# Start addresses 32 bytes further on: experts' tokens, context and the first half's query weights in SBUF

## The reference

```
x = x + latent_attention(context, layernorm(x))      # 8 heads of 128; keys and values from context and latents together
x = x + ffn(layernorm(x))                            # 256 -> 1024 -> 256, gelu, and a small term made of 16 of the tokens
x = x + cross_attention(layernorm(x), context)       # one head of 256
x = x + experts(layernorm(x))                        # 8 experts, each 256 -> 256 gate and up, silu(gate) * up, 256 -> 256 down
```

## Time and profile before

| | us |
|---|---|
| median of three executions | 1987.82 |
| lowest and highest | 1985.39, 1988.81 |
| the profiled execution: its own time | 1991.09 |
| the profiled execution: its span, first to last instruction | 1989.3 |

### The profile page before, as it was taken

The page is one execution under the profiler, slowest core; times in us unless marked ns, Lnnn a source line. Parts: engine busy times, 40 slices in busy tenths (PEclk is TensorE's granted clock), DMA queues, the critical chain, the costliest instruction groups (busy, mean ns, idle before and its releaser), DMA issues.

```text
span 1989.3 us, 41475 instructions
## 1 busy us (share of the span) xinstructions
PE 1927.2 (97%) x14078; PEld 1803.2 (91%) x14078; DVE 1367.9 (69%) x3408; ACT 1115.5 (56%) x2334; POOL 407.1 (20%) x650
## 2 busy tenths in 40 slices
PE   7999999999999999999987899999999999999998
PEld 6788888888888888888886899999999999999998
DVE  7877776776777776776746566766666666766665
ACT  5655565555655565555655655554555555544553
POOL 2222222222222222222213511111111101111100
PEclk9999999999999999999999999999999999999999
DMA  4000000000000000000012200000000000000000
GB/s 162 12 22 21 11 11 21 21 21 5 16 21 21 11 11 21 21 21 6 10 34 89 67 15 15 12 17 17 11 16 16 17 12 17 12 17 12 17 7 12
DMA packets 47211, 44.51 MB, mean 22 GB/s; under 512 B 6848, under 2 KB 45376, under 8 KB 47168
## 3 DMA queue, kind: packets, MB, share of 16 engines
q1 hardware_dynamic: 47168, 43.96, 6.9%
HBM read 34.77 MB, written 8.39 MB: 22 GB/s over the span
## 4 chain that ended last, share of the span: by engine, by line
PE 83%; DVE 7%; ACT 5%; issue 3%; POOL 1%; SPq 1%; DMA 0%; DVEq 0%; ACTq 0%; POOLq 0%
PE ring L618 9%; PE ring L620 9%; PE ring L619 9%; PE ring L1820 7%; PE ring L1818 7%; PE ring L1819 7%; PE ring L671 4%; PE sim L1818 3%; PE sim L1819 3%; PE sim L1820 3%; PE sim L618 3%; PE sim L620 2%; PE sim L619 2%; PE ps_x L1818 2%; PE ps_x L1820 2%
## 5 line engine op out<-in xcount | busy, mean ns | idle before, releaser
L411 ACT ACTIVATE a_pr<-sim,a_nmax 128x512 f32<-128x512 f32 x256 | 174.5, 689 | 208.4 <-DVE a_nmax L537 208.3
L1818 PE MATMUL ring<-b_xch,b_weh 128*128 128x256 f32 x1024 | 289.5, 283 | 1.7 <-DVE b_act_e L1464 1.7
L1819 PE MATMUL ring<-b_xcl,b_weh 128*128 128x256 f32 x1024 | 285.7, 279 | 0.0
L1820 PE MATMUL ring<-b_xch,b_wel 128*128 128x256 f32 x1024 | 285.6, 279 | 0.0
L326 POOL TENSOR_SCALAR a_pr<-a_pr,a_rinv 128x512 f32<-128x512 f32 x256 | 183.1, 729 | 498.3 <-DVE a_rinv L547 495.4
L1818 PEld LDWEIGHTS ring<-b_xch,b_weh 128*128 128x128 f32 x1024 | 192.3, 188 | 1.9 <-DVE b_act_e L1464 1.9
L1819 PEld LDWEIGHTS ring<-b_xcl,b_weh 128*128 128x128 f32 x1024 | 193.0, 188 | 0.0
L1820 PEld LDWEIGHTS ring<-b_xch,b_wel 128*128 128x128 f32 x1024 | 192.1, 188 | 0.0
L1464 DVE TENSOR_TENSOR b_act_e<-b_act_e,ring 128x512 f32<-128x512 f32 x128 | 87.9, 687 | 116.7 <-PE ring L1820 102.4
L528 DVE TENSOR_TENSOR a_ptl<-ring,a_pth 128x512 fp32r<-128x512 f32 x256 | 163.9, 682 | 3.1 <-ACT a_pth L401 2.0
L515 DVE SCALAR_TENSOR_TENSOR a_ktl<-ring,a_bkv_s,a_kth 128x512 fp32r<-128x512 f32 x128 | 95.3, 744 | 102.1 <-ACT a_kth L391 102.1
(11 more groups left out here) (378 smaller groups left out, 6246.0 us busy)
## 6 DMA issues: line engine op xcount, KB each, us to landing
a_c_in<-in_ctx_in SPq DMA_DIRECT2D x16, 256.0 KB, 2.6
a_x_in<-in_x SPq DMA_DIRECT2D x16, 256.0 KB, 2.9
a_x_res<-in_x SPq DMA_DIRECT2D x16, 256.0 KB, 2.6
x_between<-a_x_out SPq DMA_DIRECT2D x16, 256.0 KB, 2.2
b_x_s<-x_between SPq DMA_DIRECT2D x16, 256.0 KB, 2.6
b_up<-b_ev SPq DMA_DIRECT2D x256, 1.0 KB
out_x<-b_acc SPq DMA_DIRECT2D x16, 256.0 KB, 2.2
b_ct_raw<-in_ctxT SPq DMA_DIRECT2D x15, 256.0 KB, 2.6
```

The costliest lines, as they stand in the source:

```text
L411: nc.scalar.activation(pr[:, h % 2, t, :], sim[t][:], ACT.Exp, bias=nmax[:, h % 2, t:t + 1], accum_out=rsum[:, h % 2, t:t + 1]).then_inc(e ...
L1818: nc.tensor.matmul(out, lh, rh, start=(n == 0), stop=False)
L1819: nc.tensor.matmul(out, lh, rl, start=False, stop=False)
L1820: last = nc.tensor.matmul(out, ll, rh, start=False, stop=(n == len(parts) - 1 and not more))
```

## The change

`put` takes fractions of `odd`, and six tiles are put at half a step, that is 32 bytes behind a multiple of 128. Instructions, waits and their order are the same.

```
         if odd is not None:
-            self.top = (self.top - 64 * odd + 127) // 128 * 128 + 64 * odd
+            behind = int(64 * odd)
+            self.top = (self.top - behind + 127) // 128 * 128 + behind
...
-    (raw_q, wql), wqh = of["w_queries"].put("a_wql", ..., odd=1), of["w_queries"].put("a_wqh", ..., odd=1)
+    (raw_q, wql), wqh = of["w_queries"].put("a_wql", ..., odd=0.5), of["w_queries"].put("a_wqh", ..., odd=0.5)
...
-    cth, (wq_raw, ctl) = put("w_queries", "cth", ..., odd=0), put("w_queries", "ctl", ..., odd=0)
+    cth, (wq_raw, ctl) = put("w_queries", "cth", ..., odd=0.5), put("w_queries", "ctl", ..., odd=0.5)
...
-    xch, xcl = (put("values0", n, [P, DC, S], F32R, odd=0) for n in ("xch", "xcl"))
+    xch, xcl = (put("values0", n, [P, DC, S], F32R, odd=0.5) for n in ("xch", "xcl"))
```

More of the change, by code:

```diff
@@ L179, in latent_attention @@
         "a_wvl", [P, DC, INNER], F32R, raw=True, odd=0)
-    (raw_q, wql), wqh = of["w_queries"].put("a_wql", [P, DC, INNER], F32R, raw=True, odd=1), of["w_queries"].put(
-        "a_wqh", [P, DC, INNER], F32R, odd=1)
+    (raw_q, wql), wqh = of["w_queries"].put("a_wql", [P, DC, INNER], F32R, raw=True, odd=0.5), of["w_queries"].put(
+        "a_wqh", [P, DC, INNER], F32R, odd=0.5)
     (raw_k, wkl), wkh = of["w_keys"].put("a_wkl", [P, DC, INNER], F32R, raw=True, odd=1), of["w_keys"].put(
@@ L821, in ffn_attention_experts @@
         "w_queries", "wvl", [P, DC, D], F32R, raw=True, odd=1)
-    cth, (wq_raw, ctl) = put("w_queries", "cth", [P, DC, S], F32R, odd=0), put(
-        "w_queries", "ctl", [P, DC, S], F32R, raw=True, odd=0)
+    cth, (wq_raw, ctl) = put("w_queries", "cth", [P, DC, S], F32R, odd=0.5), put(
+        "w_queries", "ctl", [P, DC, S], F32R, raw=True, odd=0.5)
     once = {"K": (wk_raw, mh, ml), "Q": (wq_raw, cth, ctl), "V": (wv_raw, wvh, wvl)}
```

## The result

The changed kernel takes 1999.72 us (median of 5 runs, 1997.68 to 2003.08); the kernel before took 1987.82 beside it (5 runs, 1985.39 to 1989.78). The ratio is 1.0063, with a 95% interval of 1.0047 to 1.008: about 12 us slower, where 12 us faster had been forecast. The profiled span is 1997.9 us, against 1989.3.

What follows compares the result with a forecast made beforehand. PE's matmuls were taken as the bound: their number times the step from start to start. Terms of 10.6 + 1.7 + 1.2 + 0.3 = 13.8 us, 12 kept, gave 1979.1, or 1975.8 at the median; forecast 1976, range 1958 to 2000.

Steps and rivals of the forecast that it cites:

- slower, the phase is lost the other way: Rival for the moved products: with 32 bytes between the streams the fast phase no longer exists; middle 2000 us, chance 0.26.
- two prices, 1994 and 2012: The slower rival's times: fast strings fall to 118 ns (5.8 us), or the third, slower speed becomes the rule (24 us).
- step 1: Gate and up, tokens from 0 to 32: 2304 slow matmuls go from 117.9 to 113.3 ns, saving 10.6 us.
- step 2: First half's query weights, from 64 to 32: half of 768 matmuls are slow and become fast, saving 1.7 us.
- step 3: Context, from 0 to 32: score matmuls save 1.2 us, values at most 0.3 us.
- step 4: Neighbouring tiles that move along, such as b_act_e: DVE's product takes 687 ns and has idle time; counted as nothing.
- not the residue alone: Claim on what sets the speed: strings with the same residues modulo 128 run at 117.9 and 113.3 ns.
- The warning at the end: Matmuls of unmoved tiles (down, w1, attention's outputs) should keep their steps; if not, the sum by tiles is wrong.
- The rule weighed there: PE has two independent read ports, moving operand and weights, so the start address within 128 bytes should change nothing: 0.

Runs made afterwards that it cites:

- m1: Separate kernel without the computation: strings of equal 256-column products for every pair of starts, moving and stationary, in 32-byte steps modulo 256; steps 113.3 to 120.0 ns.
- t1: Kernel before with only the tokens b_xch and b_xcl moved to 32 bytes behind a multiple of 128; 1996.29 us, ratio 1.004.
- t3: Kernel before with only the first half's query weights a_wql and a_wqh moved to 32; 1992.45 us, ratio 1.0018.
- t8: Kernel before with the context b_cth, b_ctl at 160 modulo 256, and b_v_b, b_rt, b_wr moved with it; 1988.58 us, ratio 0.9991.
- m3: Separate kernel without the computation: strings of difference 64 or 192 chained behind strings of each difference, and other column widths; the same tiles ran at 117.8 or 113.3 ns.
- t5: Kernel before with the tokens and what lies behind them moved by a whole 128 bytes; 1985.83 us, ratio 0.9988.
- t9: Kernel before with only the second half changed: tokens at 0, weights of experts 2 and 3 at 64 modulo 256; 1982.84 us, ratio 0.9961.
- t7: Kernel before with tokens and first-half a_kvh, a_kvl at 0 modulo 256, weights of experts 2 and 3 at 64; 1986.54 us, ratio 0.9986.
- t4: Kernel before with tokens and experts' weights both 32 bytes on, neighbours as before; 1993.38 us, ratio 1.0025.
- t2: Kernel before with only the neighbours b_act_e, b_acc and b_ct_raw at 32, tokens still at 0; 1989.83 us, ratio 1.001.

## Why the prediction was wrong

It had the cost right in kind (the step, with everything else hidden behind PE), and the rival that it called "slower, the phase is lost the other way" is what happened, at the middle of that rival's price (2000; measured 1999.72). That the middle was hit is luck: it lay between two prices, 1994 and 2012, and neither came true. The slow strings did not stay at 118, as the first had it, nor did gate and up go to 123, as the second did. Its own forecast failed at these steps.

**Gate and up, step 1.** "If the new offset of 32 bytes lets them all run at the fast one" was the failing assumption. The fast speed was taken as the nearest row by kind, but a row of the old difference says nothing of a new one. The new differences have one speed each, 120.0 and 118.3 to 118.4 ns (m1, t1), and neither is 113.3. The term was -10.6 us and measured +7.3. The bound on the side of loss, 18 us, took 123 ns for every step from the score matmuls' durations; the measured means are 3 to 5 ns below that.

**Query weights, step 2.** Forecast -1.7, measured +2.7 in both the changed kernel and t3, for the same reason: from 192, of which a part is fast, to 160, of which none is.

**Context, step 3.** Forecast -1.5. Its own products lost about 1 us in the changed kernel, and 0.8 in t8, where other strings gave that back.

**The neighbours, step 4.** Right. DVE's product kept its 687 ns. Moving the neighbours alone gave 1.001, the 2 us of which no row shows.

**What sets the speed.** The prediction reasoned in residues modulo 128, as the code does, and concluded "not the residue alone" from experts 6 and 7 and from the earlier trace rows. Half of that was sound. Experts 6 and 7 do have the same difference, 192, and there history decides, as m3 shows. But the earlier trace rows do not compare equal differences: b_mh and b_w1h have the same residue modulo 128 and differ by 128 modulo 256. Working out the addresses from the regions' sizes would have shown this, and that expert 3 has another difference than expert 7. Neither would have given the speed at 160.

**The warning at the end.** "If they change, one string hands its phase to the next and my sum by tiles is the wrong account" came true: the hidden layer in t5 and t9, the attention's outputs in t7. In the changed kernel itself the moved tiles lost 11 us and all steps together 8.7. How much of that gap was handed on, to the down products for one (0.7 us), and how much is waits and the place of the clock's low stretches, was not separated.

**The rule weighed there.** By the Trainium skill, "SBUF — State Buffer", section "Who interferes with whom", PE reads moving data and weights by ports of their own. The forecast took from this that a shift by 32 bytes would be worth 0. The runs disagree with that: 1.0063 for the change, and 113.3 to 120.0 ns in m1 by the difference of the starts. The measurement decides. Nothing here says which part of the chip the two streams meet in.

**What stays open.** The mechanism: no record shows memory accesses, and that both streams meet in the same piece of memory is inferred from the cycle of 256 bytes. Why expert 3 in t9 is slow although it starts behind a stop with difference 64, as six of eight such strings in m1 were fast. Differences finer than 32 bytes were not tried. Which state a string must leave behind for the next one to be fast is not known either: m3's table is one string a cell, and m1 contradicts it as a rule. t9 gained 6.7 us where its own tiles and the hidden layer give 7.2, so little is left to explain there; how much a better order of strings could add was not tried.

## What to carry to other kernels

Where PE is back to back and one instruction form repeats, read the step from start to start, and work out the difference between the starts of weights and moving tile in full, not by the code's own residues; equal shapes with unequal steps are worth that. A difference that has one slow speed is worse than one with two, and a better difference in one string moves the strings behind it, so such an edit is tried alone and the whole loop is read again. Where a term's size hangs on a state that no row shows, its sign is unknown too, and the forecast should sit near no change.

## What the runs showed of the hardware

- The step of 256-column products from alternating high and low tiles at the full granted clock depends on the difference of starts modulo 256 bytes, from 113.3 to 120.0 ns; either start by itself does not set it (m1, t4).
- At differences 64 and 192 the speed is one of two, 113.3 or 117.8 ns, and what ran before picks it (m3, and the two passes of m1). It then holds to the string's end and can pass into the next (t5, t9). At 224 there are two as well, 116.7 and 117.8.
- At 128 columns the step is 111.7 ns whatever the difference; at 512 it varies by 3.3% (227.0 to 234.5). At 256 columns the first step behind a stop took 220 to 226 ns in 39 of m3's 40 strings, and 231 in one.
- Where the granted clock fell to 0.50 (the lower level, 1.2 GHz), steps of 113 to 120 ns became 213 to 214 (the changed kernel at 1053.9 us). Such a stretch lay elsewhere in the execution of before, so sums by tile of two traces are compared only after looking where the low stretches lie.
- DVE's 128x512 product took 685 to 687 ns wherever its tile started (before, t2, and t9, where it stands 128 bytes on).
